# Four layers fused on one core: the second attention from batch 3 on in a fixed order

## What is computed

```python
x = x + xattn_0(layernorm(x), context, ...)   # attention with one head
x = x + ffn_0(layernorm(x), ...)              # 64 slots, top 8 of them, a gated update
x = x + xattn_1(layernorm(x), context, ...)   # attention with 16 heads, then two dense layers
x = x + ffn_1(layernorm(x), ...)              # 8 experts, 2 for each row

def xattn_1(x, y):                            # the layer that this change touches
    q, k, v = (x @ Wq + bq), (y @ Wk + bk), (y @ Wv + bv)      # 16 heads of 16
    attn = softmax(einsum('bnhd,bmhd->bhnm', q, k) / sqrt(16))
    out = einsum('bhnm,bmhd->bnhd', attn, v).reshape(B, N, 256)
    return relu(out @ W1 + b1) @ W2 + b2                       # 256 -> 512 -> 256
```

## Time and profile before

| | us |
|---|---|
| median of 3 runs | 552.25 (551.52 to 552.89) |
| the profiled execution: span from its first to its last instruction | 551.1 |
| PE busy (matmuls) | 538.4, 98% |
| DVE busy | 284.0, 52% |
| ACT busy | 254.1, 46% |
| POOL busy | 168.7, 31% |
| second attention: from 181.0, the first `attend1`, to the end of `outputs1(15)` | about 147 |
| experts, from 323 on | 228 |

### The profile page before, as it was taken

How to read it: one execution, slowest core, us unless ns; L and a number is a source line. 1 busy time by engine, 2 the same in 40 slices (tenths; PEclk the granted TensorE clock), 3 DMA queues, 4 the chain that set the end, 5 groups by cost and what they waited for, 6 DMA issues and landing times.

```text
span 551.1 us, 11061 instructions
## 1 busy us (share of the span) xinstructions
PE 538.4 (98%) x3967; PEld 444.4 (81%) x3968; DVE 284.0 (52%) x847; ACT 254.1 (46%) x587; POOL 168.7 (31%) x152
## 2 busy tenths in 40 slices
PE   9999999999999999999999889999999999999995
PEld 7887878777655676777777679999999999999995
DVE  4867676988562776855788865722212111212110
ACT  1343476263346767687787834542222222222221
POOL 2211000002145222332222043354335454445533
PEclk9999999999999999999999999999999999999999
DMA  8940000000110000300470657968788888898733
GB/s 320 403 141 1 2 0 2 0 1 2 38 39 0 2 2 1 116 1 2 135 287 7 227 172 244 318 187 268 221 246 219 248 229 236 239 255 238 239 66 38
DMA packets 28651, 74.30 MB, mean 135 GB/s; under 512 B 5600, under 2 KB 20320, under 8 KB 23360
## 3 DMA queue, kind: packets, MB, share of 16 engines
q1 hardware_dynamic: 18592, 61.87, 31.9%
q0 software_dynamic: 7488, 10.39, 10.6%
q10 hardware_dynamic: 2528, 1.48, 0.9%
HBM read 62.88 MB, written 10.85 MB: 134 GB/s over the span
## 4 chain that ended last, share of the span: by engine, by line
PE 93%; ACT 4%; DVE 1%; issue 1%; POOL 0%; DVEq 0%; POOLq 0%
PE ps L897 64%; PE ps L1193 12%; PE ps L901 11%; ACT ring L617 2%; PE ps L1041 1%; PE ps L1050 1%; ACT ring L624 1%; PE ps L1053 1%; PE ps L1044 1%; PE ps L981 1%; PE ps L1024 1%; ACT HF L629 0%; ACT ring L658 0%; POOL out_x L422 0%; PE ps L1122 0%
## 5 line engine op out<-in xcount | busy, mean ns | idle before, releaser
L897 PE MATMUL ps<-keep,arena 128*128 128x128 f32 (+2 forms) x976 | 114.9, 274 | 0.0
L897 PEld LDWEIGHTS ps<-keep,arena 128*128 128x128 f32 x976 | 112.8, 192 | 1.5 <-issue 1.1
L2014 DVE TENSOR_TENSOR keep<-keep,ps 128x512 f32<-128x512 f32 x39 | 26.8, 686 | 145.7 <-PE ps L897 124.2
L422 POOL DMA_INDIRECT out_x<-arena,row_no x38 | 59.9, 1576 | 102.1 <-DMA out_x<-arena,row_no 65.2
L1193 PE MATMUL ps<-arena,keep 128*128 x312 | 73.7, 380 | 0.1
L665 ACT COPY keep<-ps 128x256 f32<-128x256 f32 x39 | 14.5, 372 | 107.1 <-PE ps L901 103.8
L381 POOL TENSOR_TENSOR ring<-arena,keep 128x512 f32<-128x512 f32 x32 | 33.5, 1049 | 96.9 <-PE ps L897 79.8
L1193 PEld LDWEIGHTS ps<-arena,keep 128*128 128x128 f32 x312 | 56.4, 190 | 6.6 <-issue 0.3
L617 ACT ACTIVATE ring<-ps,mx 128x128 f32<-128x128 f32 x192 | 52.3, 403 | 6.2 <-DVE mx L1714 6.2
L897 PE MATMUL ps<-ring,arena 128*32 128x128 f32 (+1 forms) x640 | 53.1, 348 | 1.5 <-ACT ring L624 1.4
L373 POOL TENSOR_TENSOR var_x<-var_x,minus_half 128x4 f32<-128x4 f32 x16 | 16.5, 1036 | 115.8 <-DVE var_x L1570 115.8
(11 more groups left out here) (266 smaller groups left out, 816.2 us busy)
## 6 DMA issues: line engine op xcount, KB each, us to landing
arena<-in_w SPq DMA_DIRECT2D x29, 1024.0 KB
w_first<-in_w SPq DMA_DIRECT2D x10, 1024.0 KB
arena<-in_w SPq DMA_DIRECT2D x8, 512.0 KB, 7.3
keep<-in_keep SPq DMA_DIRECT2D x1, 3115.0 KB, 20.8
ring<-in_fold SPq DMA_DIRECT2D x1, 2112.0 KB, 12.7
arena<-in_x SPq DMA_DIRECT2D x4, 512.0 KB, 10.5
arena<-in_ctxT SPq DMA_DIRECT2D x4, 512.0 KB, 7.1
arena<-in_ctx SPq DMA_DIRECT2D x4, 384.0 KB, 11.2
```

Of the source, the lines that this page charges most:

```text
L422: pool.indirect_dma_start(out=out_d, out_offset=bass.IndirectOffsetOnAxis(ap=rows_at, axis=0), in_=YO[t % DEEP], in_offset=None, compute_o ...
L897: ins = pe.matmul(out, w, m, start=(k == 0), stop=(k == len(pairs) - 1))
L2014: dve.tensor_tensor(HA[r % 2], HA[r % 2], ps[:, 2 * (r % 2) + 1, :], ALU.mult).then_inc(act_ok, 1)
```

## The change

The calls of the second attention from batch 3 on are put into another order on PE, DVE and ACT, in a repeating pattern: both scores of batch b, both attention steps of batch b-1, then the products that use the whole array (`outputs1` of batch b-2, `turn_probs1`, `hidden1` of batch b-1). On POOL two `root` calls move up by one `spread_keys`. No call is added or removed, and the functions stay as they are. Its core, by engine:

```diff
@@ on PE @@
             turn_probs1(10)
-            hidden1(3)
+            hidden1(4)
+            turn_probs1(11)
             score1(12)
-            turn_probs1(11)
-            outputs1(3)
             score1(13)
             attend1(10)
             attend1(11)
+            outputs1(4)
             turn_probs1(12)
-            hidden1(4)
+            hidden1(5)
@@ on DVE @@
+            add_outputs(2)
             shift(10)
-            add_outputs(2)
             shift(11)
             divide(4)
+            add_outputs(3)
...
             shift(24)
+            shift(25)
             route_groups(0, EB)
-            shift(25)
             divide(11)
-            shift(26)
             add_outputs(10)
             route_compare(0, EB)
+            shift(26)
+            shift(27)
             route_ties(0, EB)
-            shift(27)
             divide(12)
@@ on ACT @@
             exp1(10)
+            exp1(11)
             probs1_turned(10)
-            exp1(11)
-            hidden1(3)
+            hidden1(4)
             probs1_turned(11)
@@ on POOL @@
             spread_keys(13)
+            root(0, "xh4")
             spread_keys(14)
-            root(0, "xh4")
```

More of the change, by code:

```diff
@@ L821, in _ @@
             probs1_turned(22)
+            hidden1(10)
+            probs1_turned(23)
             exp_gate(0, EB)
-            probs1_turned(23)
             exp1(24)
-            hidden1(10)
+            exp1(25)
             probs1_turned(24)
-            exp1(25)
+            hidden1(11)
+            probs1_turned(25)
             exp1(26)
-            probs1_turned(25)
-            hidden1(11)
             exp1(27)
@@ L833, in _ @@
             hidden1(12)
+            probs1_turned(27)
             exp1(28)
-            probs1_turned(27)
             exp1(29)
             probs1_turned(28)
+            exp1(30)
             probs1_turned(29)
+            hidden1(13)
             hot_columns(1, 0)
-            hidden1(13)
-            exp1(30)
             rows4_turned(2)
+            exp1(31)
             probs1_turned(30)
-            exp1(31)
             hidden1(14)
@@ L1385, in _ @@
             turn_probs1(4)
+            outputs1(0)
+            hidden1(1)
+            turn_probs1(5)
             score1(6)
-            outputs1(0)
-            turn_probs1(5)
             score1(7)
-            hidden1(1)
-            turn_probs1(6)
-            score1(8)
             attend1(4)
@@ L1395, in _ @@
             outputs1(1)
+            turn_probs1(6)
+            hidden1(2)
             turn_probs1(7)
+            score1(8)
             score1(9)
@@ L1399, in _ @@
             attend1(7)
+            outputs1(2)
             turn_probs1(8)
-            hidden1(2)
+            hidden1(3)
+            turn_probs1(9)
             score1(10)
-            turn_probs1(9)
-            outputs1(2)
             score1(11)
@@ L1415, in _ @@
             attend1(11)
+            outputs1(4)
             turn_probs1(12)
-            hidden1(4)
+            hidden1(5)
+            turn_probs1(13)
             score1(14)
-            turn_probs1(13)
-            outputs1(4)
             score1(15)
             attend1(12)
-            hidden1(5)
             attend1(13)
@@ L1427, in _ @@
             turn_probs1(14)
+            gate_logits(0)
+            hidden1(6)
+            turn_probs1(15)
             score1(16)
-            gate_logits(0)
+            score1(17)
             attend1(14)
[L1431 to L1435, removed]
             attend1(15)
             outputs1(6)
+            turn_probs1(16)
+            hidden1(7)
             turn_probs1(17)
+            score1(18)
             score1(19)
-            hidden1(7)
-            turn_probs1(18)
             attend1(16)
             attend1(17)
+            outputs1(7)
+            turn_probs1(18)
+            hidden1(8)
+            turn_probs1(19)
             score1(20)
-            outputs1(7)
-            turn_probs1(19)
             score1(21)
-            hidden1(8)
             attend1(18)
             attend1(19)
+            outputs1(8)
             turn_probs1(20)
-            outputs1(8)
+            hidden1(9)
+            turn_probs1(21)
             score1(22)
-            turn_probs1(21)
-            hidden1(9)
             score1(23)
@@ L1462, in _ @@
             gate_logits(1)
+            hidden1(10)
+            turn_probs1(23)
             score1(24)
-            turn_probs1(23)
-            hidden1(10)
             score1(25)
@@ L1468, in _ @@
             attend1(23)
+            outputs1(10)
             turn_probs1(24)
+            hidden1(11)
+            turn_probs1(25)
             score1(26)
-            outputs1(10)
+            score1(27)
             attend1(24)
-            turn_probs1(25)
-            hidden1(11)
-            score1(27)
             attend1(25)
@@ L1488, in _ @@
             score1(30)
+            hidden1(13)
             turn_probs1(29)
-            hidden1(13)
+            score1(31)
             attend1(28)
             attend1(29)
-            score1(31)
             turn_x4(2)
@@ L2194, in _ @@
             divide(1)
+            add_outputs(0)
             shift(6)
-            add_outputs(0)
             shift(7)
-            shift(8)
             divide(2)
             add_outputs(1)
+            shift(8)
             shift(9)
             divide(3)
+            add_outputs(2)
             shift(10)
-            add_outputs(2)
             shift(11)
             divide(4)
+            add_outputs(3)
+            gather_stats(0, "xh4")
             shift(12)
-            add_outputs(3)
             shift(13)
-            gather_stats(0, "xh4")
+            norm_x4(0)
             divide(5)
+            add_outputs(4)
             shift(14)
-            norm_x4(0)
-            add_outputs(4)
             shift(15)
@@ L2217, in _ @@
             add_outputs(5)
+            gate_logits(0)
             shift(16)
-            gate_logits(0)
             shift(17)
-            shift(18)
             divide(7)
             add_outputs(6)
+            shift(18)
             shift(19)
             divide(8)
-            shift(20)
             add_outputs(7)
             gather_stats(1, "xh4")
+            shift(20)
             shift(21)
+            norm_x4(1)
             divide(9)
```

50 lines of the change are left out of this document (25 added, 25 removed).

## The result

| | before | after |
|---|---|---|
| median, us | 552.31 (551.52 to 552.89, 4 runs) | 568.85 (567.08 to 574.15, 4 runs) |
| the profiled execution: span | 551.1 | 567.6 (its own time 569.43) |
| `hidden1(0)` to `hidden1(13)` | 186.22 to 302.35 | 185.71 to 316.31 |

What follows compares the result with a forecast made beforehand. PE, 98% busy, was taken as the bound before, a chain through DVE after. Twelve batches add 16.5 us, the entry takes 2.2 back: +14.3, span 565.4, plus 1.15 gives 566.6 us; range 560 to 571.

Steps and rivals of the forecast that it cites:

- the lead: Before the change, DVE has a whole batch of time for divide ahead of hidden1, which keeps PE fed.
- The grouping: Equal kinds of product standing together on PE save 0.3 us a batch, bounds 0 and 0.35.
- The ring: Per-batch chain score, two shifts, divide, add_outputs, hidden1, transposes, through DVE: 10.13 us below unit 16, 8.83 from there.
- The table: Forecast times between successive hidden1 calls, from hidden1(1) to hidden1(13): together 124.4 us against 107.9 before, +16.5.
- The entry: At the start, hidden1(1) comes ahead of scores 6 and 7, near 192.2 instead of 194.45: -2.2 us.
- The 1.15 on top of the span: Amount by which the median lies above the profiled span, added to 565.4 to give 566.6 us.
- Behind `hidden1(13)` the delay passes on unchanged: After hidden1(13) the order is nearly the old one and the experts hang on it: +14.3 us at the end.
- Rival 1: Fewer changes of kind on PE are all that shows: eleven batches save 3.3 us, time 549; chance 0.05.
- Rival 2: Only batches up to hidden1(6) lose, DVE's extras overlapping from unit 16 on: +5.8 us, 558; chance 0.08.
- Rival 3: The clock falls in PE's waits, halving its speed for 4.0 us a batch: +48, near 615; chance 0.03.

Runs made afterwards that it cites:

- the five blocks with the lead restored: Kernel before, with the change's grouping in blocks 5 to 9, but hidden1 and outputs1 one batch further back than in the change: 552.00 us.
- The removal of 1.3: Changed kernel with BIAS_FROM 0 for 16, so DVE's subtraction and its maximum's settling fall out for odd units below 16: 563.49 us.
- the old tail with the waits filled: Changed kernel with the order of before behind scores 28 and 29, plus some transposes repeated where PE waits for add_outputs: 567.03 us.
- the profile with the old tail: Changed kernel up to scores 28 and 29, behind them the order of the kernel before on PE, DVE and ACT: 568.31 us.

## Why the prediction was right, step by step

- *PE waits for nobody before, and the lead does it.* Right. In the five blocks with the lead restored the loss is zero, with the grouping still in place. For the batches behind them the waits of PE for `add_outputs` and the added passes on DVE speak for it; there no run restored the lead.
- *The grouping saves 0.3 of PE a batch.* Right: 8.39 against 8.70 in the kernel with the lead. The pair of scores takes 1.99 by its row where one took 1.13, so about 1.92 up to the next product.
- *The ring.* Right in each term: 1.18, 1.14, 2.43, 2.00, 0.53, 2.82, together 10.10 for 10.13, and 8.80 for 8.83. The removal of 1.3 gave 1.3 (0.95 in one batch of three), the addition of a pass gave that pass where the clock held, and added work on PE cost nothing in the first four batches.
- *The table.* 124.6 for 124.4. By rows: 4-5 11.40 (11.5), 5-6 11.27 (11.1), 8-9 10.09 (10.2), 9-10 10.65 (10.4), 10-11 11.02 (11.0), 11-12 10.33 (10.3), 12-13 11.46 (11.8). That the sum is off by only 0.2 is in part luck: +0.47 in 6-7 and +0.25 in 9-10 stand against -0.34 in 12-13 and smaller ones. PE's wait ahead of `hidden1(12)` is 1.70, not over 2. One row failed in kind: 6-7, 9.30 for 8.83, where `add_bias` on POOL ran over `divide`. I had looked at POOL's `spread_keys` only.
- *The entry.* `hidden1(0)` to `hidden1(1)` took 5.98; 186.22 to the forecast 192.2 is 5.98 as well. The profiled execution reached `hidden1(0)` 0.5 earlier, for reasons ahead of the change.
- *The 1.15 on top of the span.* As a size of its own it is wrong: where a run here has both, its time lies 1.7 to 1.9 above its span (569.43 for 567.6). The profiled execution of before would then have taken some 552.9, 0.6 more than its median, and the 1.15 holds both. The forecast does not suffer: 14.3 on the median of before gives the same 566.6.
- *Behind `hidden1(13)` the delay passes on unchanged.* This is the step that was mis-sized. At `hidden1(13)` the kernel was 13.96 late, at the end 16.5. Of the 2.5, 1.5 lie before `hidden1(15)`. PE's idle time there is no longer (3.43 for 3.90), but its work takes 17.12 for 15.15. Of these 1.97, 0.97 are the transposes `turn_probs1(29)`, which the change moved from ahead of `hidden1(13)` to behind it; the prediction called the order there nearly the old one and put nothing for that. The other 1.0 goes with the clock: after the wait of 1.95 for ACT's copy of `turn_x4(2)` (1.1 before) 3.41 us run at 0.50, and `hidden1(14)` takes 3.01 where `hidden1(13)` took 1.86. Another 0.8 is a longer wait of the experts' second transposes for ACT (1.50 for 0.68). The run of the changed kernel with the highest mean clock, 567.08, is 0.5 above the forecast, and the old tail with the waits filled, 567.0, is 0.4 above it.
- *Rival 1, fewer changes of kind.* Its gain is real and is used up: the kernel with lead and grouping is no faster. The Trainium skill, TensorEngine Tiling (Array Packing), Key Properties, says that a change of the tiling mode drains the array; the trace agrees in so far as a batch with fewer such changes takes 0.31 us less of PE. It doesn't decide here.
- *Rival 2, only the batches with subtraction lose.* It did not come: from `hidden1(6)` to `hidden1(12)` the change takes 60.2 us for 53.0.
- *Rival 3, the clock.* I gave it 0.03 in its full form, and that did not come: in the twelve batches of the profile the clock stays at 1.00. A smaller form did. Drops of 3.41 us, some of twice that, follow the longer waits, in other places from profile to profile; one cost about 1.6 us in the batches where it was read.

## What to carry to other kernels

Before calls are grouped by kind, follow for each consumer how much work stands between it and its producers on every engine's list; an engine that is 50% busy can become the bound once the lead is below its chain. The sum of that chain, from start-to-start times in the old trace, gave the new batch to 0.03 us. And look also at what a third engine runs at the new time, and at what the waits do to the clock.

## What was not expected of the hardware

- The granted clock fell to 0.50 (the level of 1.2 GHz) for 3.41 us or twice that after, or still in, single waits of PE of 1.9 to 3.9 us, with PE busy up to them and behind them. The same wait of 2.76 us before `hidden1(5)` was followed by a drop in the profile with the old tail and by none in that of the change; no wait of 1.47 us was, in any profile here. The rows, timeline of PE in the changed kernel, with the moved transposes second:

```profile
316.31 2.02 PE L897 MATMUL ps<-OT,keep 128*128 128x128 f32 x16 [1.39 <-DVE routing L1824]
318.17 1.04 PE L901 MATMUL ps<-keep,ring 128*128 128x128 f32 x8
319.14 2.14 PE L897 MATMUL ps<-ring,arena 64*128 64x512 f32 x36
...
325.98 1.06 PE L901 MATMUL ps<-keep,ring 128*128 128x128 f32 x8 [1.95 <-ACT arena L634]
...
328.31 3.17 PE L897 MATMUL ps<-OT,keep 128*128 128x128 f32 x16 [0.51 <-DVE gl L2022]
```

- Transposes of data that nobody needs served to keep the clock up: with 2.6 us of them in the wait of 2.76 before `hidden1(5)` the clock stayed at 1.00, where the same wait without them was followed by a drop in one profile of three.
- DVE's L1728, with both inputs in on-chip memory, took 0.93 for 0.43 while POOL worked on two such inputs, and ended 0.29 after POOL did (252.70). It is no single case: in the profiles of this document, that of before among them, it starts 23 times while a `spread_keys` or an `add_bias` runs on POOL, takes 0.92 to 1.28, and ends 0.28 to 0.29 after that one each time. The Trainium skill, SBUF — State Buffer, SBUF: two separate sides, says that DVE and GpSimd share a pair of ports as an exclusive lock, for which a DVE instruction with two inputs in SBUF and a GpSimd instruction that reads SBUF contend: whichever starts second blocks until the first is done. The rows agree.
